# A two-layer LoRA kernel: first loads on ScalarE's queue, eight warming transposes, and a new order of VectorE's work in the loop

## The reference

```python
# x (8, 256, 1024); W0, W1 (1024, 1024)
base  = einsum('bsi,oi->bso', x, W0)
low   = einsum('bsi,bir->bsr', x, lora_A[label])        # rank 32
x = x + base + einsum('bsr,or->bso', low, lora_B_w) * 0.5
base  = einsum('bti,oi->bto', x, W1) + b
low   = einsum('bti,bir->btr', x, lora_As[slot])        # rank 16
x = x + base + einsum('btr,bro->bto', low, lora_Bs[slot]) * 2.0
```

## Time and profile before

| what | us |
|---|---|
| median of three runs (lowest, highest) | 299.31 (299.22, 299.97) |
| the profiled execution, whole | 299.78 |
| its span in the trace | 297.7 |
| TensorE busy | 291.8 |
| VectorE busy | 246.4 |
| ScalarE busy | 145.3 |
| first real matmul starts | 6.50 |
| first product of batch 2 in the steady loop to that of batch 3 | 22.84 |

### The profile page before, as it was taken

One profiled execution on the slowest core, in us unless ns is written; L12 is line 12 of the kernel. 1 busy time (PEld: TensorE's weight loads), 2 busy tenths in 40 slices (PEclk: granted clock), 3 DMA queues, 4 the chain that ended last, 5 costly groups with the idle time before them and its releaser, 6 DMA issues.

```text
span 297.7 us, 4279 instructions
## 1 busy us (share of the span) xinstructions
PE 291.8 (98%) x1336; PEld 241.1 (81%) x1336; DVE 246.4 (83%) x366; ACT 145.3 (49%) x239; POOL 24.0 (8%) x52
## 2 busy tenths in 40 slices
PE   7999999999999999999999999999999999999996
PEld 6788888888888888788778888888888888888885
DVE  3489997989999999999998897897887987985432
ACT  3585576879257646354434534434435425435100
POOL 1733000010010500000100000000000000000000
PEclk9999999999999999999999999999999999999999
DMA  6999520900006400183462642552462462011012
GB/s 171 302 312 342 74 37 1 142 0 2 0 0 108 71 0 1 22 156 123 72 152 87 111 109 88 89 131 88 79 141 87 77 144 87 10 68 73 1 37 107
DMA packets 99507, 27.57 MB, mean 93 GB/s; under 512 B 84901, under 2 KB 93349, under 8 KB 99494
## 3 DMA queue, kind: packets, MB, share of 16 engines
q1 hardware_dynamic: 99494, 27.41, 39.9%
HBM read 19.01 MB, written 8.39 MB: 92 GB/s over the span
## 4 chain that ended last, share of the span: by engine, by line
PE 62%; DVE 22%; issue 7%; ACT 3%; DMA 2%; POOL 1%; SPq 1%; DVEq 0%; ACTq 0%; POOLq 0%
PE bank L1145 60%; DVE xt L914 3%; DVE vt_lo L671 3%; DVE s_sum L671 2%; DMA a<-in_L_cond_W 2%; PE bank L1168 2%; DVE vt L671 2%; DVE s_lo L671 2%; DVE v L671 2%; DVE v_lo L671 1%; DVE t_lo L671 1%; DVE lhs L671 1%; ACT s_hi L435 1%; DVE u_sum L671 1%; DVE p_lo L671 1%
## 5 line engine op out<-in xcount | busy, mean ns | idle before, releaser
L1145 PE MATMUL bank<-v_hi,lhs 128*128 128x512 f32 (+1 forms) x136 | 42.8, 378 | 0.4 <-DVE u_st L671 0.4
L1145 PE MATMUL bank<-vt_hi,s_hi 128*128 128x512 f32 x96 | 37.3, 389 | 0.0
L1145 PE MATMUL bank<-vt_lo,s_hi 128*128 128x512 f32 x96 | 37.3, 389 | 0.0
L1145 PE MATMUL bank<-vt_hi,s_lo 128*128 128x512 f32 x96 | 37.3, 389 | 0.0
L914 DVE STREAM_TRANSPOSE xt<-raw 128x512 int32<-128x512 int32 x32 | 33.5, 1083 | 0.2
L1145 PEld LDWEIGHTS bank<-v_hi,lhs 128*128 128x128 f32 x136 | 25.2, 188 | 5.5 <-issue 0.8
L435 ACT ACTIVATE lhs<-xt 128x512 fp32r<-128x512 f32 x32 | 19.8, 629 | 16.1 <-PE bank L1145 15.7
L435 ACT ACTIVATE s_hi<-s_sum 128x512 fp32r<-128x512 f32 x32 | 19.0, 622 | 14.4 <-PE bank L1145 11.6
L1145 PE MATMUL bank<-v_lo,lhs 128*128 128x512 f32 (+1 forms) x68 | 25.8, 380 | 0.0
L435 ACT ACTIVATE u_st<-u_sum 32x256 fp32r<-32x256 f32 x24 | 10.0, 417 | 26.8 <-DVE u_sum L671 26.6
L671 DVE TENSOR_TENSOR lhs<-xt,lhs 128x512 fp32r<-128x512 f32 x32 | 21.7, 686 | 0.5
(11 more groups left out here) (163 smaller groups left out, 653.1 us busy)
## 6 DMA issues: line engine op xcount, KB each, us to landing
raw<-in_x SPq DMA_DIRECT2D x32, 256.0 KB, 4.8
out<-y SPq DMA_DIRECT2D x31, 256.0 KB, 2.1
n<-in_L_cond_W SPq DMA_DIRECT2D x16, 256.0 KB, 6.1
a<-in_L_cond_W SPq DMA_DIRECT2D x16, 256.0 KB, 5.7
a_raw<-in_L_cond_lora_A SPq DMA_DIRECT2D x8, 128.0 KB, 2.3
a_raw<-in_L_cond_lora_As SPq DMA_DIRECT2D x8, 64.0 KB, 2.4
b_raw<-in_L_cond_lora_Bs SPq DMA_DIRECT2D x8, 64.0 KB, 2.0
out<-y SPq DMA_DIRECT2D x2, 128.0 KB, 1.9
```

Source lines behind the costliest of these rows:

```text
L1145: return nc.tensor.matmul(ps, lhsT, rhs, start=start, stop=stop, skip_group_check=more)
```

## The change

Five edits:

- a11's first piece and the two index loads are issued by ScalarE at the beginning of its program, not by SP.
- `warm_up(8)` replaces `warm_up(10)`.
- VectorE, batches 1 to 6: transposes 0, 1 and 2 stand together ahead of u2; u_total comes directly behind u2 (but for the wait), transpose 3 behind u_total; then u0_low and b1_low; next_sums 0 stands where next_sums 1 was, and next_sums 1 behind u_low and ahead of a_low 0. In batch 7, b1_low moves behind u0_low too.
- ScalarE, batches 1 to 6: s_high 0 and 1 stand behind u_hi, not ahead of it.
- batch 0's order is as it was.

```diff
@@ SyncE
             for j in range(HK):
                 load_n(n11, 0, 0, j, n11_in[j])
-                load_a(a11, 0, 0, j, a11_in[j])
-                if j == 2:
-                    sp.dma_start(index[0:1, 0:B], label0.rearrange("(o b) -> o b", o=1)).then_inc(index_in, 16)
-                    sp.dma_start(index[0:1, B:2 * B], slot1.rearrange("(o b) -> o b", o=1)).then_inc(index_in, 16)
+                if j > 0:
+                    load_a(a11, 0, 0, j, a11_in[j])
@@ ScalarE, start
+            first_a = w0.rearrange("(b j p) (a i) -> p b j a i", b=2, p=P, a=2)[:, 0, 0, 0, :]
+            act.dma_start(a11[:, 0, :], first_a).then_inc(a11_in[0], 16)
+            act.dma_start(index[0:1, 0:B], label0.rearrange("(o b) -> o b", o=1)).then_inc(index_in, 16)
+            act.dma_start(index[0:1, B:2 * B], slot1.rearrange("(o b) -> o b", o=1)).then_inc(index_in, 16)
@@ ScalarE, batch
                 if not (first or final):
                     a_high(b + 1, 2)
+                act.wait_ge(h_made, b + 1)
+                copy(u_st[32:64, :], u_sum[32:64, :], u_hi_made)
+                if first:
+                    a_high(b + 1, 2)
+                elif not final:
                     act.wait_ge(m5_done, b + 1)
                     s_high(b + 1, 0)
                     act.wait_ge(m6_done, b + 1)
                     s_high(b + 1, 1)
-                act.wait_ge(h_made, b + 1)
-                copy(u_st[32:64, :], u_sum[32:64, :], u_hi_made)
-                if first:
-                    a_high(b + 1, 2)
@@ VectorE, batch
                     if not final:
                         dve.wait_ge(s_sum_made, 4 * b + 4)
-                        turn_next(b + 1, range(2))
-                    b1_low(b)
-                    if not final:
-                        turn_next(b + 1, range(2, 3))
+                        turn_next(b + 1, range(3))
...
-                    if not final:
-                        turn_next(b + 1, range(3, 4))
                     dve.wait_ge(u_lo_made, b)
                     u_total(b)
                     if not final:
-                        next_sums(b + 1, 0)
+                        turn_next(b + 1, range(3, 4))
                     u0_low(b)
+                    b1_low(b)
...
                 elif not final:
-                    next_sums(b + 1, 1)
+                    next_sums(b + 1, 0)
...
                 elif not final:
+                    next_sums(b + 1, 1)
                     a_low(b + 1, 0)
@@ TensorE
-            warm_up(10)
+            warm_up(8)
```

## The result

| | before | changed |
|---|---|---|
| median of the runs, us | 299.50 (22 runs, 298.69 to 300.29) | 300.58 (22 runs, 299.22 to 301.75) |
| ratio of the changed kernel to before | | 1.0034, 95% interval 1.0024 to 1.0044 |
| median span, us | 297.3 | 297.55 |
| median time outside the span, us | 2.1 | 3.0 |
| profiled execution: time, span, rest | 299.78, 297.7, 2.1 | 300.31, 297.4, 2.9 |

The spans and times outside of the kernel before are those of its 104 runs beside the experiments (22 runs of it are the median above). The changed kernel is slower by 0.34%, just beyond what can be told from no change, and outside my range of 296.8 to 299.1. The table already splits the miss: 0.9 us of it lies outside the span, a place for which I had no term, and within the span the gain of 1.6 us isn't there.

A forecast was written before the change was run, and what follows sets the result against it. TensorE, busy 98% of the span, was taken as the bound, with only its pauses to win. Loop 1.1 + start 0.5 = 1.6 us, taking the median from 299.31 to 297.7 us; range 296.8 to 299.1.

The forecast's parts named there:

- the gain of 1.6 us: Whole kernel: 1.1 us from the loop in batch 1 plus 0.5 us from the start.
- Loop, batch 1: Batch 1: earlier u0_low and u_low remove TensorE's pauses, taken as 1.1 us of 1.19.
- Both waits: Batch 1, TensorE: 0.59 us before v21's product and 0.40 us before the low-rank step, both released by u_st.
- One step of the working: Batch 1: TensorE comes to the low-rank weights 3.35 - 0.82 = about 2.7 us after 146.12, at 148.8.
- Loop, steady batches: Batches 2 to 6: u_low ends at 172.57, 0.24 us before the weight load at 172.81; costed at nothing.
- Rival D: Steady batches: VectorE's chain exceeds 6.40 us, u_low comes after the weight load; 301.0 us at 0.8 us lateness; chance 0.07.
- the failed step: Start: both first tiles flow together, n11's landing some 0.4 us later at about 4.1, the other at about 4.2.
- rival B: Start: gives all that the DMA rows allow, 1.2 us, for 297.0 us; chance 0.10.
- rival C: Start: TensorE's clock rises later, some 15 matmuls at twice their time; +1.9 us, 299.6; chance 0.08.
- that pause is under 0.5 us: Start: TensorE's idle time from about 3.7 until n11 lands, claimed under 0.5 us against the late clock.
- the pause ahead of 6.50: Start: a 1.49 us TensorE pause before the first real matmul, claimed to do no harm.
- The 0.5 us of gain: Start: GpSimd's add at 11.43 comes 0.5 us earlier, as SP's queue loses a11's first tile's 0.49 us issue.

The follow-up runs named there:

- e1: Kernel before with only the new order of VectorE and ScalarE in the loop; loads and ten warming transposes as before: 298.50 us, ratio 0.9971.
- e4: Kernel before with only the two index loads moved to ScalarE's queue: 299.49 us, ratio 1.0005.
- e12: Changed kernel with the first tiles' queues exchanged (n11's on ScalarE's, w0's on SP's) and twelve warming transposes: 298.39 us, ratio 0.9959.
- e5: Changed kernel with fourteen warming transposes instead of eight in the first group: 298.26 us, ratio 0.9956.
- e6: Changed kernel with ScalarE issuing the two index loads ahead of w0's first tile: 301.46 us, ratio 1.0083.
- e9: Kernel before with the new loop order and eight warming transposes, loads as before: 299.29 us, ratio 0.9991.
- e14: e1 with two transposes instead of four in the second warming group: 299.52 us, ratio 0.9997.
- e13: Changed kernel with eight already fulfilled waits added on TensorE behind the eight warming transposes: 300.09 us, ratio 1.0014.
- e2: Kernel before with only the start's part (new loads, eight warming transposes), old loop order: 301.03 us, ratio 1.0052.
- e3: Kernel before with only warm_up(8) instead of warm_up(10): 299.20 us, ratio 1.0005.
- e8: Changed kernel with the two index loads back on SP's queue: 301.02 us, ratio 1.0041.
- e7: Changed kernel with eight more waits on SP, on loads landed by then: 301.14 us, ratio 1.0051.
- e15: e1 with ten transposes instead of four in the second warming group: 298.52 us, ratio 0.9968.
- e16: Changed kernel with 14 and 8 warming transposes instead of 8 and 4: 298.56 us, ratio 0.9967.
- e11: Changed kernel with six transposes instead of four in the second warming group: 299.58 us, ratio 1.0001.
- e10: Changed kernel with ten warming transposes instead of eight in the first group: 299.35 us, ratio 0.9983.

## Why the prediction was wrong, step by step

**Loop, batch 1: right.** Both waits are gone, 12.56 of 12.56; forecast 1.1 us, the traces' distance changes by 1.1, e1's ratio gives 0.9 (0.5 to 1.2). One step of the working doesn't add up: 3.35 - 0.82 is 2.53, not "about 2.7"; the 2.7 stands on batch 2's 2.68 alone, and nothing else changes by it. **Loop, steady batches: right.** Slack 0.20 us where 0.24 was forecast, no pause in 150.06 to 287.00; VectorE's idle time ahead of y's last quarter shrank from 1.74 to 0.81. Rival D didn't happen.

**Start: the failed step.** It is the sentence "Both first tiles then flow together from the beginning: n11's tile lands some 0.4 us later than now, at about 4.1". It landed at 5.07. The issue time was cut as forecast, and it bought the DMA engines more work in the first 5 us (177 GB/s against 131, or against 151 in e1 and 158 in e4); the pieces for GpSimd came 1.5 us earlier than in the earlier trace rows, even more than rival B's 1.2, but only 0.9 earlier than in e1 (10.78). But the first tile that TensorE needs is n11's, and I had asked what the load that was moved would gain and not what it would take from the one that it now runs beside. The Trainium skill, "DMA: Bandwidth & Descriptors", section "Issuing engines are not separate DMA queues", says that such loads run on the same 16 engines and interleave. The trace agrees in so far as n11's tile landed at 5.07 instead of 3.69 with the other load beside it, but the first two tiles didn't interleave to a common end: they landed 0.75 us apart, in the same order with the queues exchanged (e12).

**From there rival C took over**, which I had given 0.08. It named the mechanism (TensorE idle until n11 lands, the clock rises late) and was argued away with "that pause is under 0.5 us", which rests on the failed step. The pause was 1.24 us. Sized at +1.9 us by some 15 slow matmuls, it was less here: e5 against the changed kernel gives 297.55 - 296.2 = 1.35 us in the span. My second reason, that the pause ahead of 6.50 did no harm, was true but of another place: in that trace the clock had risen at 4.51, before the pause (which is 1.17 us by the earlier trace rows, not the 1.49 of the prediction).

**The 0.5 us of gain was no gain either**, even with the clock mended: e5 lies 0.24 us and e12 0.11 us below e1, within the intervals. The earlier trace rows had caught w0's tile 1 us later than four of the six other traces with the same loads have it, so part of what I meant to win wasn't lost in those.

**The time outside the span: a missing term.** I took it as fixed at 2.1. It is 3.0 in the median of the changed kernel.

The account by medians: the kernel before, 297.3 + 2.1; the loop, -0.9 (e1); the start, +1.15 (the changed kernel's span against e1's); outside, +0.9; sum 300.6, measured 300.58. Of the miss of 2.9 us, 0.9 are the time outside, and the start accounts for 1.15 that it cost and 0.5 that it was to give; the rest is the loop's 0.2 and a median of before that came out 0.2 higher.

## What to carry to other kernels

When a load is moved to start earlier, price what it takes from the load that the first consumer waits for, not only what it gains; here the tile needed second overtook the tile needed first. A pause of TensorE shortly after the start, before its clock has risen, can cost more than its length: fill it up to the landing of the data (14 transposes for 8, 1.35 us here), and judge a warming by when it ends against when the data lands. Compare the time of an execution with its span before explaining a small difference, since part of it may lie where no instruction is.

## What the runs showed of the hardware

- Time outside the span gathers at two places, 2.04 to 2.23 us and 2.85 to 3.79 (seven runs lie between, at 2.30 to 2.56), and a kernel can show both from run to run. The long one appeared only with the new loop and with TensorE's program shorter than before by two instructions (the changed kernel, e6 to e9, e14), and never with eight more waits on TensorE (e13, 0 of 12). The same eight transposes with the old loop (e2, e3) didn't bring it, so the count isn't the whole condition. In the five profiled executions with the long time (the changed kernel, e6, e8, e9 and e14) the last 16 KB fetch of instructions comes 2.2 us behind the end of the span (299.65, 298.6, 299.7, 298.0 and 299.5); in most with 2.1 us outside it comes before the end (292.9 before the change, 291.2 in e1, 296.6 in e13), though e2 has one 1.1 us behind its span. e7 shows both times from run to run; its profiled execution was a short one, with the fetch at 291.7. This goes together with the long time, and no run here shows that it causes it.
- The moment at which TensorE's clock reaches the full level differs from trace to trace (one execution each): 4.4 to 4.8 us in before, e3, e4 and e6, 6.3 to 7.5 in e1, e5, e9, e12, e15 and e16, 8.4 to 10.0 in the changed kernel, e7, e8, e11 and e14, 10.9 to 11.4 in e2, e10 and e13. e1 has before's start in every instruction of TensorE and rose at 6.37, not at 4.51, so part of this is chance. With 1.16 to 1.34 us of idle time ahead of n11's tile (the changed kernel, e2, e7, e8, e11, e13) it was never before 8.4, and the first four products took 0.43 to 0.47 us each; within these the length doesn't decide, as e2 with 1.20 us was slower than the changed kernel with 1.24. With 0.75 us (e10) the spans go either way. With none or 0.37 us it was at most 7.5, but for e14.
- The later rise shows in the span: the matmul behind n22's first turned tile starts at 15.95 to 16.78 us where the clock rose by 7.5 (17.20 in e16, whose added transposes held up the products), at 17.14 to 17.65 where it rose at 8.4 to 10.0, and at 18.34 to 18.63 where it rose later. The granted clock in the view of stretches stays at 1.00 in most of them; only the starts of the matmuls show it.
